# Attention scores of a decoder layer: one group of four score products per batch in place of two pairs

## The reference

```
x = layernorm(x + mamba(x))                        # two directions, 256 channels, 16 states
x = layernorm(x + cross_attention(x, ctx, ctx))    # 16 heads of 8 channels, 128 queries x 128 keys
x = layernorm(x + moe(x))                          # 8 experts, top 1, capacity 160, relu between

# cross attention, per batch b
Q, K, V = x @ Wq.T, ctx @ Wk.T, ctx @ Wv.T
scores  = einsum('bqhd,bkhd->bhqk', Qh, Kh) / sqrt(8)
out     = softmax(scores) @ Vh  ->  concatenated heads @ Wo.T
```

## Time and profile before

| | |
|---|---|
| median of the runs (three) | 337.58 us (337.52 to 338.89) |
| the profiled execution, its own time | 339.48 us |
| its span, first to last instruction | 337.7 us |
| busy share of the span | PE 91%, DVE 86%, ACT 75%, POOL 59% |
| chain that ended last | PE 44%, DVE 31%, issue 9%, POOL 8% |
| mean granted TensorE clock | 0.97 of full speed |
| score products, L1002 | 64 records, 18.0 us together, mean 639 ns |
| maximum L1397 and subtraction L1402 | 16 each, 19.5 us each, mean 1.22 us |

### The profile page before, as it was taken

How to read it: one execution, slowest core, us unless ns; L and a number is a source line. 1 busy time by engine, 2 the same in 40 slices (tenths; PEclk the granted TensorE clock), 3 DMA queues, 4 the chain that set the end, 5 groups by cost and what they waited for, 6 DMA issues and landing times.

```text
span 337.7 us, 5762 instructions
## 1 busy us (share of the span) xinstructions
PE 308.3 (91%) x1814; PEld 194.1 (57%) x1814; DVE 289.9 (86%) x499; ACT 253.4 (75%) x471; POOL 198.1 (59%) x134
## 2 busy tenths in 40 slices
PE   6999989899999999899999999999999998699980
PEld 5544558466655565454445444565656657598970
DVE  2788887999999999999999999977978989680583
ACT  2669998998999989899999999965777677312431
POOL 7500619999999998889898898431100001550244
PEclk9999959999999999999999999999999999989996
DMA  6996212132333332313323210000000000015010
GB/s 157 313 297 216 80 63 64 62 125 72 117 100 94 112 95 102 124 62 126 95 94 123 69 59 1 0 3 0 2 0 2 2 1 2 19 47 143 9 35 22
DMA packets 15377, 26.23 MB, mean 78 GB/s; under 512 B 1971, under 2 KB 8908, under 8 KB 15348
## 3 DMA queue, kind: packets, MB, share of 16 engines
q1 hardware_dynamic: 14580, 24.76, 23.4%
q0 software_dynamic: 768, 1.11, 1.1%
HBM read 23.49 MB, written 2.51 MB: 77 GB/s over the span
## 4 chain that ended last, share of the span: by engine, by line
PE 44%; DVE 31%; issue 9%; POOL 8%; ACT 3%; DMA 3%; SPq 1%; DVEq 0%; POOLq 0%; ACTq 0%
DVE arena L1303 23%; PE bank L756 16%; POOL arena L456 6%; PE bank L1002 5%; PE bank L800 4%; DVE acc L1313 4%; PE bank L898 3%; PE bank L1021 2%; PE bank L822 2%; PE bank L1171 2%; PE bank L1163 2%; PE bank L788 2%; DMA cw<-in_L_attn_convb_w 1%; PE bank L911 1%; PE bank L945 1%
## 5 line engine op out<-in xcount | busy, mean ns | idle before, releaser
L456 POOL TENSOR_TENSOR arena<-arena,k_maskT 128x1024 f32<-128x1024 f32 x64 | 150.4, 2375 | 37.0 <-DVE arena L1290 19.3
L1303 DVE TENSOR_TENSOR_SCAN arena<-bank,arena 128x512 f32<-128x512 f32 x128 | 146.3, 1208 | 0.0
L756 PEld LDWEIGHTS bank<-ident,arena 128*128 128x128 f32 x718 | 77.9, 141 | 79.4 <-DVE arena L1303 51.4
L756 PE MATMUL bank<-ident,arena 128*128 128x128 f32 x718 | 103.8, 281 | 13.3 <-DVE arena L1303 7.4
L898 PE MATMUL bank<-conv_in_T,ident 128*128 128x512 f32 x192 | 93.4, 595 | 0.1
L562 ACT ACTIVATE bank<-delta,a_neg 128x508 f32<-128x508 f32 x128 | 88.2, 692 | 6.1 <-DVE arena L1303 5.3
L608 ACT ACTIVATE conv_in_T<-bank,c_col 128x256 f32<-128x256 f32 x192 | 80.3, 472 | 9.9 <-PE bank L756 9.0
L898 PEld LDWEIGHTS bank<-conv_in_T,ident 128*128 128x128 f32 x192 | 31.5, 191 | 15.8 <-issue 15.6
L468 POOL TENSOR_SCALAR rstd<-moments 128x4 f32<-128x4 f32 (+1 forms) x5 | 1.2, 235 | 56.1 <-DVE moments L1356 56.1
L1313 DVE SCALAR_TENSOR_TENSOR acc<-bank,c_col,acc 128x256 f32<-128x256 f32 x64 | 27.6, 476 | 2.2 <-PE bank L756 2.0
L674 ACT ACTIVATE arena<-bank 128x1024 f32<-128x1024 f32 x16 | 16.4, 1023 | 12.4 <-PE bank L756 12.4
(11 more groups left out here) (174 smaller groups left out, 333.7 us busy)
## 6 DMA issues: line engine op xcount, KB each, us to landing
k_maskT<-b_rows SPq DMA_DIRECT2D x32, 512.0 KB, 3.7
w_sb<-in_L_ffn_w SPq DMA_DIRECT2D x1, 2048.0 KB, 10.4
dispatched_tokens<-zeros SPq DMA_DIRECT2D x1, 650.0 KB, 17.8
x_tok<-in_x SPq DMA_DIRECT2D x1, 512.0 KB, 4.0
ctx_tok<-in_ctx SPq DMA_DIRECT2D x1, 512.0 KB, 4.4
out<-uT SPq DMA_DIRECT2D x1, 512.0 KB, 4.5
arena<-dispatched_tokens SPq DMA_DIRECT2D x2, 130.0 KB, 2.3
arena<-dispatched_tokens SPq DMA_DIRECT2D x1, 260.0 KB, 3.6
```

The source lines that it names most:

```text
L456: gp.tensor_tensor(dBx[g % 2][h], du[:, dr, h, :], b_bc[:, g % RING, :], ALU.mult).then_inc(dBx_ok, 1)
L756: return pe.transpose(dst, src, ident[0:src.shape[0], 0:src.shape[0]])
L1303: ve.tensor_tensor_scan(o, a, v, 0.0, ALU.mult, ALU.add).then_inc(scanned, 1)
```

## The change

The scores of a batch are computed in one go. `scores(b)` issues four products, on four row groups into banks 0 to 3, and hands over the first pair of banks behind the second product and the other behind the fourth. It stands in odd loop steps only, behind `turn_probs(i - 1)`, for the next batch. It can be filled only when both halves of the batch before were read. On VectorE the residual of batch i // 2 - 3 and its moments move behind the second subtraction of the same odd step, ahead of `normalize_values`. The amount of arithmetic is the same.

```diff
--- before.py
+++ after.py
@@ -233,8 +233,8 @@
         plan += [("s0", 0, 2), ("s1", 2, 2), ("yTC0", 7), ("yTC1", 6)]
         BETWEEN = {1: [("x1TB", 6), ("oC", 7), ("qB", 6)], 3: [("v1", 7)], 4: [("x1TC", 7)], 5: [("qC", 7)]}
         for i in range(2 * B):
-            if 1 <= i < 2 * B - 1:
-                plan += [(f"s{i + 1}", 2 * ((i + 1) % 2), 2)]
+            if i % 2 == 1 and i < 2 * B - 1:
+                plan += [(f"s{i + 1}", 0, 2), (f"s{i + 2}", 2, 2)]
             plan += BETWEEN.get(i, [])
             if i % 2 == 1 and i >= 5:
                 plan += [(f"avq{i // 2 - 2}", 7)]
@@ -992,16 +992,18 @@
             pe.wait_ge(moe_w_in, 48)
             filled("centred", pe.matmul(to_fill(pe, "centred")[:, 0:E], centre[:, :], gate[:, :], start=True, stop=True))
 
-            def scores(i):
-                b, c = i // 2, i % 2
-                to_fill(pe, f"s{i}")
+            def scores(b):
+
+                for c in range(2):
+                    to_fill(pe, f"s{2 * b + c}")
                 pe.wait_ge(masks_ok, GH * (b // HB) + GH)
                 wait_read(pe, f"q{'AABBCCCC'[b]}")
-                for g in (2 * c, 2 * c + 1):
+                for g in range(HEADS // GH):
                     in_g = slice(GH * DH * g, GH * DH * g + GH * DH)
                     last = pe.matmul(bank[:, g, :], qT[in_g, S * b:S * b + S],
                                      k_maskT[in_g, b, :, :].rearrange("p j k -> p (j k)"), start=True, stop=True)
-                filled(f"s{i}", last)
+                    if g % 2:
+                        filled(f"s{2 * b + g // 2}", last)
 
             def turn_probs(i):
                 pe.wait_ge(exp_ok, i + 1)
@@ -1082,14 +1084,11 @@
             pe.wait_ge(v_zero, 2)
             scores(0)
             add_part(last_g, 2)
-            scores(1)
             for k in (1, 2):
                 wait_read(pe, f"y{k}")
             for h in range(NH):
                 turn_group(f"yTC{h}", [y_rows(b, h) for b in range(*PARTS["C"])])
             for i in range(2 * B):
-                if 1 <= i < 2 * B - 1:
-                    scores(i + 1)
                 if i == 5:
                     queries("C")
                 if i % 2 == 0 and i >= 6:
@@ -1100,6 +1099,8 @@
                     turn_x1("B")
                     project_y("C")
                     queries("B")
+                if i % 2 == 1 and i < 2 * B - 1:
+                    scores(i // 2 + 1)
                 if i == 4:
                     turn_x1("C")
                 if i == 2 * B - 1:
@@ -1396,8 +1397,6 @@
                 steps[0] += 1
                 ve.tensor_reduce(rmax[:, c, :], src, AX.X, ALU.max).then_inc(dve, 1)
                 max_done = steps[0]
-                if i % 2 == 1 and i >= 7:
-                    add_residual(i // 2 - 3)
                 ve.wait_ge(dve, max_done)
                 was_read(f"s{i}", ve.tensor_tensor(prob[i % 3], src, rmax[:, c, :].unsqueeze(2).to_broadcast([P, CH, S]),
                                                    ALU.subtract))
@@ -1476,11 +1475,11 @@
                     normalize(res1, x1, 0, 2, *PARTS["C"], x1_ok)
                 if i == 2 * B - 1:
                     evacuate("raw0", rawT[:, half(0)])
+                if i % 2 == 1 and i >= 7:
+                    add_residual(i // 2 - 3)
+                    end_batch(i // 2 - 3)
                 if i % 2 == 1 and i >= 5:
                     normalize_values(i // 2 - 2)
-                if i % 2 == 0 and i >= 8:
-                    end_batch(i // 2 - 4)
-            end_batch(B - 4)
             normalize(res2, x2, 1, 0, *ROUTES[0], x2_ok)
             choose_expert(0)
             place_tokens(0)
```

## The result

The changed kernel is slower by more than was forecast: 348.48 us (median of 4, 348.06 to 349.16) against 338.20 on the same chip, a ratio of 1.030 (95% interval 1.028 to 1.032), +10.3 us. The forecast was 344.1 us with a range of 341.8 to 348.0: the sign was right, the size was not, and the time lies outside the range. The forecast stood on a median of 337.58 us for the kernel before, of three runs; with a fourth it is 338.20. Of the 4.4 us between forecast and result, 0.6 are this shift.

What follows compares the result with a forecast made beforehand. TensorE was taken to bound the kernel by 0.7 us a batch; 3.5 us at maximum 6, four batches at +0.83, -0.5 in the last and +0.2 behind it gave +6.5, hence 344.1 us, range 341.8 to 348.0.

Steps and rivals of the forecast that it cites:

- What bounds: Steady part: TensorE bounds the stage by only 0.7 us a batch over VectorE; a longer new serial wait takes over.
- The price of a quad: TensorE's four score products at once: 1.06 us, as for a pair, with 2.12 as the other end.
- Quads that run two by two: Rival at the four score products: row groups run side by side only in twos, +7.4, 351.5 us; chance 0.06.
- The ring: Each steady batch: subtraction, four products, value transposes, normalization and four VectorE steps follow without overlap, 7.21 us, 0.83 more.
- The first batches: Batches 1 to 3, losing the second bank pair: maximum 2 1.75 us late, maximum 4 2.1, maximum 6 3.5.
- the last batch: Last batch, with no four products behind it: its four steps take 4.86 us instead of 5.37, 0.5 off the delay.
- the moved work's cover: VectorE's moved residual and moments, under 0.8 us with their link, cost nothing inside its 1.85 us wait for turned values.
- the sum: Whole stage: 3.5 at maximum 6, 6.8 at maximum 14, 6.3 after the last batch, +0.2 for the residual: +6.5 us.
- The clock falls: Rival in the steady part: TensorE's granted clock falls for a batch or a little more, +3 to +4, 347.5 us; chance 0.06.
- The walk of batch 2: Batch 2: subtraction 3 ends at 245.93, then 0.15, 1.13 and 0.04 put maximum 4 at 247.25, 2.1 us late.
- The residual releases the bank of the value transposes: VectorE's moved residual frees that bank at about 0.4 us, long before the four products end, so it delays nothing.
- the walk: The prediction's step-by-step delays from first batches to the end of the stage: 2.1, 3.5, 6.8, 6.3 and finally 6.5 us.

Runs made afterwards that it cites:

- both gaps filled: Changed kernel with step 15's residual ahead of VectorE's copy, and 13 and 20 idle transposes on TensorE in the two gaps before batch 2's four products: ratio 1.021.
- the early residual: Changed kernel with the residual of each odd step ahead of VectorE's copy of the turned residuals, which exists in step 15 only; moments stay behind: ratio 1.026.

## Why the prediction was wrong

- *What bounds* was right: TensorE's relief of 8.5 us did not arrive, since the quad closed a ring between TensorE and VectorE.
- *The price of a quad*: 1.06 forecast, 1.07 measured. Quads that run two by two did not occur. The Trainium skill, "TensorE: Matmul & The Clock Gate", section "Measured speedup vs the span model", gives 3.07 times the rate, by which the estimate was 1.12 us; here four products of 0.86 ran in 1.07, 3.2 times the rate, so the trace is slightly better.
- *The ring*: 7.21 forecast, 7.23 measured. Subtraction to quad took 0.10 where I put 0.15, quad to reciprocal 0.69 where I put 0.64.
- *The first batches, the last batch, the moved work's cover*: maxima 2, 4, 6 and 14 and the last subtraction fit within 0.1 us, once the clock is held (both gaps filled).
- *The failed step* is the sum without a term for the clock. "The clock falls" stood among the rivals at 0.06, and I looked for its cause in the ring, where TensorE is busy for 78% (22.46 of 28.92; I reckoned 73%) and nothing fell in this kernel. Its price of +3 to +4 us was worked out for a fall there, with 5.29 us doubled taken as about 10 (it is 10.6); that it lies near the 2.7 is luck. The walk of batch 2 itself had a quad that starts 0.15 us behind subtraction 3, at 246.1, while TensorE's work ahead of it ends long before; I never computed that gap. It is 2.6 us, with another of 2.06 ahead of the half before, and the fall at these gaps cost 2.7 us in the changed kernel's profile and 1.5 in that with the early residual. All four profiles that leave both gaps open fell by 6.8 us there. Of the five that leave the first at 2.06 and fill the second, with idle or real work, two fell for 3.4 us and three did not. Of the six in which the first gap is 1.49 us or less, the kernel before among them, none fell there.
- *A second step failed*: "The residual releases the bank of the value transposes, at about 0.4 us, long before the quad ends." That holds in the steady part. In step 15 there is no quad, and a copy that waits for TensorE stands ahead of the residual. At 1.0 us it was a term that had to be in the sum.
- The size: 6.5 from the walk, 2.7 for the clock, 1.0 for the residual are 10.2 of the 10.3 us. Either term alone would have left the time inside the range, and so, by 0.1 us, would both on the median of 337.58 that the forecast started from.

What stays open: what decides whether the clock falls where only the first gap is open, and when a fall begins, on which its price hangs (1.5 or 2.7 us). One execution of each kernel was profiled, so how often the other runs fell is not known either.

## What to carry to other kernels

When a group of products takes all buffers, its start hangs on the last reader, and everything in the list between it and that reader's next work becomes one ring: add up the ring, and put only work there that the other engine waits for last. Then compute, for every place where such a wait is new, how long the waiting engine is idle; for TensorE two gaps of 2.06 and 2.6 us close together were enough for the clock to fall to half in all four profiles, which cost another 1.5 to 2.7 us, and the first alone was enough in two of five. And look at first and last steps of a loop by themselves: a move that is covered in the steady part had a copy ahead of it in the last step.

## What the runs showed of the hardware

Four products over 32 partitions each, on four row groups and four banks, held TensorE for 1.07 us where two held it for 1.06: the second pair adds 0.01. (What the prediction calls two passes are the two records that each product leaves.)

The granted clock fell to 0.50 at gaps of 2.06 and 2.6 us with about 1.1 us of work between them. In three profiles the fall began in the second gap, in the fourth (early residual) 0.2 us behind the end of the first. It stayed low for 6.8 us in all four, and for 3.4 us in the two that fell with the second gap filled. Filling the second gap with idle transposes kept the clock up in one kernel and not in another with the same list at that place. No profile fell there with the first gap at 0.43, 0.54 or 1.49 us.
